# Channel coefficients of a hybrid convolution, attention and expert kernel: made in two batches, the first inside the interpolation loop, the second during attention

## What is computed

```python
x = x + deformable_conv(group_norm(x))          # 9 taps, bilinear interpolation by learned offsets
g = group_norm(x)
pooled = rms_norm(mean over positions of g)      # per image
c = pooled @ phi_w.T + phi_b                     # 24 numbers per image
H_pre, H_post = sigmoid(a * c[:4]), 2 * sigmoid(b * c[4:8])
H_res = exp(d * c[8:]).reshape(4, 4)
for _ in range(20):                              # Sinkhorn
    H_res = H_res / H_res.sum(-1); H_res = H_res / H_res.sum(-2)
x = x + mean over streams of (H_res @ g + H_post * conv3x3(sum(H_pre) * g))
t = tokens(x)                                    # 8 images x 256 tokens x 64
t = t + causal_attention(layer_norm(t))          # 8 heads
t = t + experts_of_8(layer_norm(t), top 2)       # hidden 256, gelu
t = t + windowed_gate(layer_norm(t))
t = t + experts_of_16(layer_norm(t), top 2)      # hidden 128, silu
```

## Time and profile before

| | |
|---|---|
| median of 3 runs | 493.99 us (492.98 to 494.06) |
| the profiled execution | 493.35 us |
| its span in the trace | 490.9 us |
| mean granted clock of TensorE | 0.985 of full |
| TensorE matmul busy | 438.3 us (89%) |
| VectorE busy | 343.7 us (70%) |
| ScalarE busy | 278.1 us (57%) |
| GpSimd busy | 155.8 us (32%) |

### The profile page before, as it was taken

The page is one execution under the profiler, slowest core; times in us unless marked ns, Lnnn a source line. Parts: engine busy times, 40 slices in busy tenths (PEclk is TensorE's granted clock), DMA queues, the critical chain, the costliest instruction groups (busy, mean ns, idle before and its releaser), DMA issues.

```text
span 490.9 us, 8869 instructions
## 1 busy us (share of the span) xinstructions
PE 438.3 (89%) x2982; PEld 299.1 (61%) x2982; DVE 343.7 (70%) x1029; ACT 278.1 (57%) x667; POOL 155.8 (32%) x189
## 2 busy tenths in 40 slices
PE   2997999968986999999999999999998987998994
PEld 2686777743534899889998944344444543544542
DVE  3278798528885867797878863636667878787763
ACT  1567666432215898888888866666664233343431
POOL 4400000000230738276223342425251454353342
PEclk9999999997999999999999999999999999999998
DMA  8200000000040032100000004212112121131330
GB/s 196 122 2 1 2 0 1 1 1 1 0 85 1 3 85 51 39 1 1 3 1 2 1 22 132 57 32 71 39 56 76 46 89 66 35 130 43 95 102 11
DMA packets 13324, 20.91 MB, mean 43 GB/s; under 512 B 4480, under 2 KB 6144, under 8 KB 12768
## 3 DMA queue, kind: packets, MB, share of 16 engines
q1 hardware_dynamic: 13136, 20.25, 14.3%
q10 hardware_dynamic: 144, 0.11, 0.1%
HBM read 19.62 MB, written 0.72 MB: 41 GB/s over the span
## 4 chain that ended last, share of the span: by engine, by line
PE 60%; DVE 22%; ACT 7%; issue 6%; POOL 2%; DMA 2%; POOLq 0%; SPq 0%; DVEq 0%; ACTq 0%
PE PS L1829 13%; PE PS L1573 7%; PE PS L1589 6%; PE PS L1840 5%; PE PS L1851 5%; PE PS L1753 3%; PE PS L1765 3%; PE PS L1665 2%; DVE M L1094 2%; PE PS L1534 2%; PE PS L1678 2%; PE PS L1712 2%; PE PS L1781 2%; PE PS L1782 2%; ACT score_arena L777 2%
## 5 line engine op out<-in xcount | busy, mean ns | idle before, releaser
L1829 PE MATMUL PS<-YTs,WH 64*128 64x512 f32 x192 | 78.0, 432 | 2.9 <-ACT VV L877 2.3
L1829 PE MATMUL PS<-YX,WH 64*128 64x512 f32 x192 | 78.3, 432 | 0.0
L575 POOL TENSOR_TENSOR pr<-pr 128x512 f32<-128x512 f32 x39 | 50.3, 1289 | 83.8 <-DVE pr L1339 53.4
L777 ACT ACTIVATE score_arena<-score_arena,nmx 128x128 f32<-128x128 f32 (+1 forms) x128 | 56.9, 446 | 13.7 <-DVE nmx L1291 13.1
L877 ACT ACTIVATE VV<-PS 128x512 f32<-128x512 f32 x64 | 35.3, 594 | 42.0 <-PE PS L1829 41.9
L1829 PEld LDWEIGHTS PS<-YTs,WH 64*128 64x128 f32 x192 | 35.8, 187 | 30.9 <-ACT VV L877 12.5
L1450 DVE TENSOR_TENSOR stage<-VV,PS 128x512 f32<-128x512 f32 x64 | 41.8, 682 | 17.7 <-ACT VV L877 14.2
L832 ACT ACTIVATE stage<-PS,wk 128x512 f32<-128x512 f32 x64 | 40.8, 684 | 21.2 <-PE PS L1829 20.9
L718 ACT ACTIVATE st_mem<-PS 128x512 f32<-128x512 f32 x72 | 36.5, 614 | 21.6 <-PE PS L1589 21.6
L1047 DVE TENSOR_TENSOR prod<-hats 128x768 f32<-128x768 f32 x48 | 42.5, 951 | 0.1
L1829 PEld LDWEIGHTS PS<-YX,WH 64*128 64x128 f32 x192 | 35.8, 187 | 4.3
(11 more groups left out here) (232 smaller groups left out, 1073.8 us busy)
## 6 DMA issues: line engine op xcount, KB each, us to landing
QH<-gate_store SPq DMA_DIRECT2D x96, 128.0 KB, 2.9
stage<-in_wexp SPq DMA_DIRECT2D x6, 512.0 KB, 6.1
wk<-in_w SPq DMA_DIRECT2D x1, 1034.0 KB, 7.8
wa<-in_wat SPq DMA_DIRECT2D x1, 768.0 KB, 6.1
cst<-in_consts SPq DMA_DIRECT2D x1, 611.0 KB, 6.5
X<-in_x SPq DMA_DIRECT2D x2, 256.0 KB, 5.2
out<-X SPq DMA_DIRECT2D x16, 32.0 KB, 1.9
wc<-in_w SPq DMA_DIRECT2D x2, 183.5 KB, 5.8
```

The source lines that it names most:

```text
L575: nc.gpsimd.tensor_tensor(acc[:, c % 2], acc[:, c % 2], weighted[:, u % 2], ALU.add).then_inc(acc_added, 1)
L777: ins = nc.scalar.activation(PR[:, s % 3, cols], MS[:, s % 3, cols], ACT.Exp, bias=nmx[:, s % 3, qt:qt + 1], scale=-1.0, accum_out=rsum[:, ...
L1829: ins = mm(PS[:, banks[i], :], w[hs, m, tiles[i] * P:(tiles[i] + 1) * P], ys[i][hs, cs], start=(k == 0), stop=(k == 2))
```

## The change

- Start: X is loaded in eight transfers, four from SP and four from ScalarE's queue; the first 256 columns of the constants are a transfer of their own. WO is split before the group norm ends. ScalarE makes GHP from X with bias and scale. Two `keep_awake` products in place of four.
- The coefficients are made for two batches, `BATCHES`: image pairs one and two (b = 0), and three and four (b = 1). Batch 0: TensorE's three small products stand at taps 23, 26 and 29 of the loop (`PE_GROUP`, `PE_SQUARE`, `PE_COEF`), VectorE's steps between its hat products, ScalarE's norm and exponential after taps 26 and 28. The sigmoids become exponential, add one and reciprocal. `prods` has four buffers; `x1_image` of pair one and two comes after units 5 and 8. VectorE starts the half iterations of batch 0 after the last hat product and puts the statistics of pairs three and four and copies of batch 1 between them. The last product of the 40th half goes into one instruction with the trace.
- Batch 1's norm and coefficients are made by GpSimd, after the loop. Its half iterations 0 to 9 are VectorE's, at three places before the first attention step; halves 10 to 39 are made during attention steps 0 to 16: GpSimd makes the sums in two additions and the product, VectorE the reciprocal (`inverse`), once between the two masks of a step and once at its end. The trace follows on GpSimd; the coefficient of the diagonal comes through bank 7 ("cB", step 18), the second residual of pairs three and four at step 19.
- The scaled convolution is added to X1 by VectorE in one instruction from PSUM, with the bias put in by ScalarE. The convolutions stand between other products, at places that `keep_awake` had or near them. AVL is made by repeating the weight products on top of a product with minus identity and AVH, and copied by ScalarE, which waits for `av_taken`. The first layer norm takes its root on ScalarE.
- The weight splits move to steps 25, 33 and 41, the norms of chunks 2 and 3 about four steps later, the folds of images 0 and 1 to step 19.
- Experts: some two dozen small pieces move by one unit or change places with a neighbour.

The diff, cut:

```diff
+DIAG_AT, XT_AT, YA_AT = 18, (20, 27), (7, 25, 38)
+DVE_HALVES = 10
+POOL_HALVES = tuple(min(40, DVE_HALVES + 2 * s - (s > 3) - (s > 4)) for s in range(19))
+MID_INVERSE, END_INVERSE = [s for s in range(17) if s != 4], [s for s in range(15) if s != 3]
...
+    if s == DIAG_AT:
+        out.append(("cB", 0))
...
+X1_AT = (5, 8)
+HAT_AT = {2: (1, 0), 5: (1, 1), 9: (2, 0), 11: (2, 1), 15: (3, 0), 17: (3, 1)}
+VARIANCE_AT, SQUARE_AT, MEAN_AT, POOLED_AT, LOGITS_AT = (9, 1), (9, 3), (10, 1), (10, 3), (11, 1)
+HALVES = (8, 20, 25, 30, 36)
...
+PE_GROUP, PE_SQUARE, PE_COEF = 23, 26, 29
+ACT_LOAD, ACT_NORM, ACT_EXP = 24, 26, 28
...
-            prods = [tensor(early, f"prod{n}", PT * 2, TRIPLE, S) for n in range(2)]
+            prods = [tensor(early, f"prod{n}", PT * 2, TRIPLE, S)[:] for n in range(3)]
+        prods.append(Y2[:].rearrange("p t c -> p (t c)").rearrange("p (b k q) -> p b k q", b=2 * PT, k=TRIPLE))
...
-            for h in range(2):
-                sp.dma_start(X[h * C:(h + 1) * C], x[h * J:(h + 1) * J].rearrange("j c s -> c j s")).then_inc(x_loaded, 16)
-            sp.dma_start(cst[:], consts).then_inc(const_loaded, 16)
+            for j in range(J):
+                sp.dma_start(X[0:C, j], x[j]).then_inc(x_loaded[j], 16)
+            sp.dma_start(cst[:, 0:2 * P], consts[:, 0:2 * P]).then_inc(mean_loaded, 16)
...
+            def half_steps(lo, hi):
+
+                for n in range(lo, hi):
+                    view = sinkhorn_views(1)[n % 2]
+                    if n == DVE_HALVES:
+                        pool.wait_ge(balanced, 2)
+                    step(nc.gpsimd.tensor_tensor(mh[0:B, 1], view[:, :, 0:2], view[:, :, 2:4], ALU.add))
+                    settle()
+                    sums = nc.gpsimd.tensor_tensor(mn[0:B, 1].unsqueeze(2), mh[0:B, 1, :, 0:1], mh[0:B, 1, :, 1:2], ALU.add)
+                    if assisted(n):
+                        sums.then_inc(sums_ready, 1)
+                        pool.wait_ge(inverse_ready, sum(assisted(m) for m in range(DVE_HALVES, n + 1)))
+                    else:
+                        step(sums)
+                        settle()
+                        step(nc.gpsimd.tensor_tensor(mn[0:B, 1], mn[0:B, 1], neg_one[0:B].to_broadcast([B, STREAMS]), ALU.pow))
+                        settle()
+                    step(nc.gpsimd.tensor_tensor(view, view, mn[0:B, 1].unsqueeze(2).to_broadcast([B, STREAMS, STREAMS]), ALU.mult))
+                    settle()
...
+            batch_gates(0)
+            batch_moments(1)
+            batch_norm(1)
+            batch_pooled(1)
+            batch_logits(1)
+            batch_gates(1)
...
+                if 0 <= s < len(POOL_HALVES) - 1:
+                    half_steps(POOL_HALVES[s], POOL_HALVES[s + 1])
+                if s == len(POOL_HALVES) - 1:
+                    trace()
...
-                if s in (5, 13, 29):
-                    split_stage((5, 13, 29).index(s))
+                    fold(pr8[:, 2 * (n % 2):2 * (n % 2) + 2], HEADS * C, slice(2 * n, 2 * n + 2))
+                if s in SPLIT_AT:
+                    split_stage(SPLIT_AT.index(s))
...
+            for j in range(J):
+                act.dma_start(X[C:2 * C, j], x[J + j]).then_inc(x_loaded[j], 16)
...
+                nc.scalar.activation(GHP[:, j, 1:HH + 1, 1:WW + 1], img(X)[:, j], ACT.Identity, bias=small[:, 12 + j:13 + j],
+                                     scale=small[:, 4 + j:5 + j]).then_inc(ghp_ready, 1)
...
+                if i in HAT_AT:
+                    hat(*HAT_AT[i])
+                if i == ACT_LOAD:
+                    nc.scalar.activation(small[:, 44:44 + J], c_("euler"), ACT.Exp).then_inc(exp_loaded, 1)
+                if i == ACT_NORM:
+                    batch_apply(0)
+                if i == ACT_EXP:
+                    batch_exp(0)
+            batch_bias(0)
...
             act.wait_ge(av_ready, 1)
-            for to in (AVH[:], av):
-                nc.scalar.activation(to[:, 0:1024].rearrange("p (a n) -> p a n", a=2), PS[:, 4:6, :], ACT.Copy).then_inc(avh_ready, 1)
-                nc.scalar.activation(to[:, 1024:1536].rearrange("p (a n) -> p a n", a=2), PS[:, 6:8, 0:256], ACT.Copy).then_inc(avh_ready, 1)
+            copy_av(AVH, avh_ready)
+            batch_apply(1)
+            batch_exp(1)
+            act.wait_ge(av_taken, 1)
+            copy_av(AVL, avl_ready)
+            nc.scalar.activation(small[:, 40:40 + J], c_("euler"), ACT.Sqrt).then_inc(table_loaded, 1)
+            act.wait_ge(lnvar_ready, 1)
+            nc.scalar.activation(lnst[:, 1, 0:4], lnst[:, 1, 0:4], ACT.Sqrt).then_inc(ln_sd_ready, 1)
+            act.wait_ge(table_loaded, 2)
+            nc.scalar.activation(small[:, 44:44 + J], c_("euler"), ACT.Exp).then_inc(table_loaded, 1)
+            batch_bias(1)
...
+            half_steps(0, 0, 4)
+            gate_inverse(0)
+            half_steps(0, 4, HALVES[0])
+            x1_image(2)
+            half_steps(0, HALVES[0], HALVES[1])
+            x1_image(3)
+            half_steps(0, HALVES[1], HALVES[2])
+            copy_group(1)
+            half_steps(0, HALVES[2], HALVES[3])
+            copy_square(1)
+            half_steps(0, HALVES[3], HALVES[4])
+            copy_logits(1)
+            half_steps(0, HALVES[4], 2 * SINKHORN)
...
+            half_steps(1, 0, 2)
+            gate_inverse(1)
             take_tokens(0)
-            ln_stats(0)
-            for j in range(1, J):
-                second_residual(j)
+            ln_center(0)
+            ln_variance(0)
             ln_out(0, False)
+            second_residual(1)
+            half_steps(1, 2, 4)
             ln_evac("yA", 0)
+            add_conv(2)
+            add_conv(3)
...
+            half_steps(1, 4, DVE_HALVES)
             take_tokens(1)
...
+                if s in MID_INVERSE:
+                    inverse()
...
+                if s == DIAG_AT + 1:
+                    second_residual(2)
+                    second_residual(3)
...
+                if s in END_INVERSE:
+                    inverse()
...
                         top_first("gD", 2, E3)
+                        ln_low(3)
                         top_second(E3)
-                    if r == 11 and i == 0:
-                        ln_low(3)
...
-            keep_awake(1, 4, 2 * P)
+            keep_awake(1, 2, 2 * P)
...
+                if i == PE_GROUP:
+                    group_means(0)
+                if i == PE_SQUARE:
+                    square_means(0)
+                if i == PE_COEF:
+                    coefficients(0)
...
+            spread_gates(0)
...
+            conv(0, 0, 4)
             pe.wait_ge(x1_tile_ready, J)
-            pe.wait_ge(moments_ready, 2)
...
-            conv(0)
...
-            conv(1)
...
-            keep_awake(2, 8, 4 * P)
+            group_means(1)
+            attention_weights(False).then_inc(av_ready, 1)
+            conv(0, 4, 5)
+            square_means(1)
+            conv(0, 5, TAPS)
+            coefficients(1)
+            pe.wait_ge(minus_ready, 1)
+            pe.wait_ge(avh_ready, 2)
+            attention_weights(True)
+            for n, (bank, width) in enumerate(((4, 512), (5, 512), (6, 256), (7, 256))):
+                at = 512 * n if n < 2 else 1024 + 256 * (n - 2)
+                ins = mm(PS[:, bank, 0:width], minus, AVH[:, at:at + width], start=False, stop=True)
+            ins.then_inc(av_taken, 1)
             pe.wait_ge(v3_diag_ready, 1)
-            mm(PS[:, 0, 0:J], spread, V3[0:B, :, 0], start=True, stop=True).then_inc(cb_ready, 1)
+            mm(PS[:, 0, 64:66], spread, V3[0:B, 0, BATCHES[0], 0], start=True, stop=True).then_inc(cb_diag_ready, 1)
+            conv(1, 0, 1)
...
+                else:
+                    pe.wait_ge(conv_added, J)
...
-            keep_awake(2, 5, 4 * P)
+            conv(1, 1, 6)
+            spread_gates(1)
+            conv(1, 6, 7)
             transpose_y("yA", 0)
-            pe.wait_ge(avl_ready, 1)
+            conv(1, 7, TAPS)
...
```

605 lines of the change are left out of this document (396 added, 209 removed), and 2 rows, old and new, of the table FIRST_FILLS.

## The result

| | before | after |
|---|---|---|
| median of 20 runs each | 493.75 us | 490.77 us (486.73 to 494.27) |
| the profiled execution | 493.35 us | 486.73 us, the fastest of its runs |
| its span | 490.9 us | 484.9 us |

The ratio is 0.9936, 95% interval 0.9915 to 0.9958: 3.0 us faster, where 15.8 were forecast, and outside the range. Over the 20 executions the span goes from 484.9 us at a mean granted clock of 0.982 to 492.4 us at 0.964, so the profiled execution had the highest clock of them, and the median is the figure to keep.

What follows compares the result with a forecast made beforehand. TensorE was busy 89% of the span, but hardly mattered from 105.8 to 155.4 us, where Sinkhorn on VectorE stood in the chain. From 493.35 us, -1.5 + 1.6 - 16.4 + 3 - 2.5 = -15.8 gave 477.6, range 470 to 486.

Steps and rivals of the forecast that it cites:

- Front: Start up to the offset convolution: loads in pieces and shorter path start it earlier; -1.5 us, bounds -3.4 to +0.5.
- up to 1.5 us go back: Start: with two of four warming products gone, part of the earlier products would run near the 1.2 GHz level.
- Loop: Interpolation loop: three small products added 1.1 us and a wait at tap 26 0.5; +1.6, bounds +0.6 to +3.6.
- rule on the exclusive lock: Loop: GpSimd and two-input VectorE instructions exclude each other; squares 1.1 us later, sum +2.7 instead of +1.6, time 478.7.
- Gap: Last tap to first attention mask: 20 Sinkhorn halves go under the loop, AVL's copy is late next; -16.4 us, bounds -18 to -13.
- Attention, hand-overs: Attention steps 0 to 16: half the inverses between Pool and VectorE are paid; +3 us, bounds -1 to 18.
- Rival D: Attention: each of 30 hand-overs costs its full 1.15 us round, 34.5 in place of 3; 509 us, chance 0.05.
- The step that failed: Attention: later folds, splits, biases and residuals of pair three and four go to steps with Pool idle; nothing.
- Experts: The two expert networks: new orders recover some of TensorE's idle time; -2.5 us, bounds -8 to +3.
- three signs of a wrong prediction: Mask 18 over 45 us after mask 0, first mask later than 143, or experts changed by over 5 us.
- Rival B: Attention and experts: handshake paid at 0.3 for each of 30 (9), orders bring nothing; 486.0 us, chance 0.17.

Runs made afterwards that it cites:

- skip_halves: Changed kernel with half iterations 10 to 39 of image pairs three and four left out; 484.16 us.
- old_places: As skip_halves, with tokens, norms, biases, folds and weight splits at the attention steps where the kernel before has them; 478.5 us.
- eased: Changed kernel with four warming products, first weight split at step 22, coefficients' product alone in step 18, chunk 0's norm one step earlier; 483.18 us, timed again 482.64.
- after_again: The changed kernel, unchanged, measured and profiled anew; 490.67 us, ratio 0.9938 to the kernel before.
- awake_and_split: Changed kernel with four warming products instead of two ahead of the offset convolution, and the first weight split at step 22 instead of 25; 491.28 us.
- experts_as_before: Changed kernel with TensorE's fillers of the experts' units in the order of the kernel before, VectorE's order kept new; 490.32 us.
- filled_waits: Changed kernel with spare TensorE products in its waits, three in step 20 and five in step 30; 488.04 us.
- cb_alone: Changed kernel with the second batch's coefficients' product alone in step 18, projections moved around it, pair four's residual at step 22; 484.22 us.

## Why the prediction was wrong, step by step

- **Front** -1.5 forecast. The convolution started at 11.99 instead of 13.80, near the 12.3 named, but lasted 11.56 instead of 10.08; its end moved by 0.3 us. The step "up to 1.5 us go back" was nearly the whole of it, in after's two profiles. (The stretch of the earlier trace rows that the prediction took for an idle TensorE has it busy for 5.63 of 6 us: it shows the clock behind a pause, which is what mattered here too, where TensorE was idle for 2.94 us ahead of the convolution.)
- **Loop** +1.6 forecast, +0.6 measured: the last tap ended at 106.10 instead of 105.79, with the loop beginning 0.3 earlier. No break of TensorE at tap 26. The Trainium skill's rule on the exclusive lock ("SBUF — State Buffer", section "SBUF: two separate sides"), by which the sum would have been +2.7, didn't show in the loop: beside the power at 80.02 (1.36 us) the two products of hats at 79.86 took 1.82 us together, no more than the 0.951 each of the earlier trace rows. Beside the weight split a product with two SBUF inputs took 0.61 instead of 0.43, but the casts with one input took longer too, 0.37 and 0.48 instead of 0.29, so these rows don't show that the rule is the reason.
- **Gap** -16.4 forecast, -17.6 from last tap to first mask. The chain of after goes as the prediction laid it out, with AVL's copy next in line and six half iterations ahead of the mask:

```profile
121.23 1.02 ACT AVL L920
122.25 0.50 ACT AVL L921
...
122.89 0.41 PE PS L1987 x2
...
132.09 0.75 PE PS L2013 x4
...
137.62 0.18 DVE ef L1293
```

143.12 became 122.89 (123.2 forecast), 150.70 became 132.09 (131.9), the mask 138.15 (139.0).
- **Attention, hand-overs** +3 forecast, +3.9 in steps 0 to 18, and skip_halves shows all of it to be the half iterations and their hand-overs (4.0). A round is 1.03 us (1.15 forecast), and since two of them are 2.06, no step of 6 to 15 is shorter, where before has steps of 1.15 and of 2.8. That half of the inverses would be paid was a guess between wide bounds, and that it came within 1 us is partly luck. Rival D's price is not paid: 4.0 / 30 = 0.13 us per hand-over, far below its 0.63.

```profile
142.43 0.19 POOL L645 TENSOR_TENSOR mn<-mh 8x4 f32<-8x4 f32 x1
142.90 0.20 POOL L654 TENSOR_TENSOR ef<-ef,mn 8x16 f32<-8x16 f32 x1 [0.28 <-DVE mn L1306]
143.18 0.20 POOL L643 TENSOR_TENSOR mh<-ef 8x8 f32<-8x8 f32 x1
143.46 0.19 POOL L645 TENSOR_TENSOR mn<-mh 8x4 f32<-8x4 f32 x1
```

- **The step that failed** is the sentence "The later folds, splits, biases, and the residuals of pair three and four (2 x 0.50) go to steps with Pool idle; nothing." The term was put at 0 and measured 9.2 us: 8.4 in steps 18 to 36 and 0.8 in steps 36 to 63. The pieces didn't only need Pool, and Pool wasn't always idle for them: the power of chunk 3 stood behind the weight split. The coefficient took bank 7 in a step that also projects through it, the residuals stood in VectorE's queue between a wait and the mask, the norms met in step 29, and the projections of image four moved two steps and met a transposition in bank 7. It was priced by the engine that does it and should have been priced by what is shared: the bank, the queue behind it, and the slot that it leaves to the next piece. The same work at before's places costs 9.5 us less in steps 18 to 36 and 3.7 more in steps 0 to 18 (old_places against skip_halves), and eased took back 5.5 of the 8.4 by five small moves: most of it was places. Not all of it: at before's places attention still took 3.9 us more than before. Of the 8.4, 1.8 came by way of the lower clock behind the two waits.
- **Experts** -2.5 forecast. The profiles say -1.8, but before's has one stretch of low clock there and after's none, which is worth 1.5. The gain of the stage is 0.2 to 0.5; the term was a guess without a row, as the prediction said.
- **Sum.** With +9.2 in place of 0 for the places and 0 for the experts, the forecast would have been 489.3. The median is 1.5 above that. The clock behind mask 63 can make such a difference (one stretch), and after's typical execution has a lower granted clock (mostly 0.971 to 0.976) than its profiled one (0.982); that it is the cause of just these 1.5 us is an estimate.

None of the rivals named the places of moved work, and none of the three signs of a wrong prediction came true (mask 18 came 40.3 us after mask 0, the first mask at 138.15, the experts changed by 1.8): no sign stood on the steps behind 18, where the loss was. Rival B came nearest in time (486.0), by another mechanism.

## What to carry to other kernels

Work that is moved off the critical path into a full schedule isn't free because its engine is idle: list for each piece the bank, the queue and the slot that it takes, and who stands behind it. When moves are tried one at a time and none pays, try them together before giving them up, and read the granted clock of each: here three edits gave -1.6, +1.6 and +0.1 us from mask 18 to mask 36, and together -5.5, with a low clock behind a wait in each single one and none in all together. Cut a schedule that is written by hand by the start of its steps; stages with the same code agreed within about 1 us over all kernels here where the clock was alike, and within 1.8 where it wasn't, while the total wanders by 7 from run to run.

## What the hardware showed that was not expected

The same wait of TensorE was sometimes followed by a lower granted clock and sometimes not. Two profiles of one kernel, the same wait for a norm near 360 us, first after, then after_again, timeline and window of each:

```profile
362.46 0.66 PE L1998 MATMUL PS<-cst,Y 128*128 128x128 f32 x4 [2.10 <-DVE Y L1438]
```

```profile
360.00:365.00 5.00, 2.90 (x18) 1.42 (x18) 2.03 (x2) 2.92 (x4) 2.05 (x3) 1.00 0.45 136
```

```profile
362.12 1.11 PE L1998 MATMUL PS<-cst,Y 128*128 128x128 f32 x4 [2.11 <-DVE Y L1438]
```

```profile
360.00:365.00 5.00, 2.89 (x9) 1.01 (x8) 1.29 (x1) 2.45 (x4) 1.78 (x2) 0.71 0.44 155
```

The wait is 2.10 and 2.11 us; the transposes behind it took 0.66 us at full clock and 1.11 at the 1.2 GHz level. Each such stretch cost about 1.5 us of the time, and the count of them (0 and 3) accounts for the 4.7 us between the two profiles of one kernel. The Trainium skill, "TensorE: Matmul & The Clock Gate", section "HAM oscillation — how this bites in real kernels", tells of waits that send TensorE back to the low clock each time; the trace agrees that it happens behind waits, but here it was not each time. The wait of 1.80 us in step 20 was followed by a clock of 0.74 over 186 to 190 us in after, and by 1.00 in awake_and_split (1.79 us). The wait of 3.01 us in step 30 was followed by 1.00 in experts_as_before, while after's, of 2.97, was followed by 0.60 over 212 to 216 us.

The low clock isn't always a cost. In steps 24 to 36 a clock of 0.60 against 1.00 over 212 to 216 changed 0.2 us (after, filled_waits); down for about twice as long it cost 1.8 (cb_alone, skip_halves). In steps 18 to 24 0.86 against 1.00 over 188 to 200 changed 1.6 us.

The front has the same spread. The offset convolution, 36 products, took (first product to the first of what follows) 10.5 to 11.7 us in the ten profiles with two warming products, and 9.3, 9.3 and 11.2 in the three with four; before, also with four, had 9.9. So four are likely better, by about a microsecond, but three executions of the same front that differ by 1.9 don't settle it.
